# The warp's offsets stored as one-byte integers

## The chip, the cores and the metric

One core of a Trainium2 chip. The metric is the device time of one execution, in microseconds.

## What is computed

The input is x, 128 images of 64 x 256. Four layers follow one another, each x + ffn(cond(x)):

```python
x = x + _L0_ffn_ref(_L0_cond_ref(x, dx, angle), ...)      # rigid transform of each image, ternary-weight FFN
x = x + _L1_ffn_ref(_L1_cond_ref(x, ..., ids), ...)       # masked attention, mixture of 4 experts, 2 per row
x = x + _L2_ffn_ref(_L2_cond_ref(x, ids, ...), ...)       # language adapter and layer norm, frequency-domain product
x = x + _L3_ffn_ref(_L3_cond_ref(x, ids, W, b), ...)      # per-category product, gated ternary-weight FFN
```

The change concerns the rigid transform alone. Each output pixel is read at a rotated and shifted place with bilinear weights:

```python
ix = (yp / h * 2.0 + 1.0) * 0.5 * (w - 1);  iy = (xp / w * 2.0 + 1.0) * 0.5 * (h - 1)
out = gather(iy0, ix0) * (wy0 * wx0) + gather(iy0, ix1) * (wy0 * wx1)
    + gather(iy1, ix0) * (wy1 * wx0) + gather(iy1, ix1) * (wy1 * wx1)
```

## The kernel before

The 128 images are worked in 32 quarters of 4 (QI = 4, NQ = 32). A quarter goes through four parts on the same engines: the front (warp, FFN of layer 0, attention and router of layer 1), the experts (rows sorted by expert, in ten blocks of quarters), the back (adapter, layer norm, frequency product) and the last part (category product, gated FFN). On each engine these parts are threads of instructions; `weave` merges them in an order that is written out by hand as a string per engine (`ORDER`). An engine works its string strictly in that order, and engines wait for one another by semaphores.

The warp of one image runs like this. An image is cut into groups of GJ x GI = 4 x 8 = 32 output pixels, so that a pixel of a group is one of 32 places k. For each group a window of the padded input is gathered by GpSimd into SBUF (`w_win`, line 1158, four indirect DMAs an image). Inside a window, place k of every group of an image reads a 3 x 3 patch at one offset, the same for all groups. The 32 offsets of an image are the array `w_offsets`: `shift[k]` is row shift times WY plus column shift, with WY = 4, computed once for all images.

In `prepare`, VectorE computes the offsets of all images with the image index on the partition (line 424) as an array of PX = 32 integers; SyncE stores it to DRAM (`offD`, line 334). In `network`, SyncE reloads the 128 offsets of a quarter into partition 0 of `woff[par]` (`load_offsets`, line 586), in two buffers by turns, with semaphore `s_off`. In thread `warp(q)` (lines 762 to 795) VectorE's sequencer loads the 32 offsets of one image into 32 of its registers with one TENSOR_LOAD (lines 770 to 773), and then issues 32 multiplications (line 780), one for each place k, whose input address is `shift[k] + a * IWIN` from the register; a short register operation (FUSED_REGOPS) goes ahead of each. After that come the sums over the patch (lines 784, 785, 789, 790, 795). Between groups of 8 multiplications, and between the sums, the written order takes VectorE to instructions of the other threads. The registers are rewritten for the next image.

Two more loads of VectorE and the others into registers are of single integers: the expert's column (line 983 on VectorE, 1327 on ScalarE, 630 on SyncE), all of four bytes.

Of the kernel before, what the change touches and what calls it, by code (L numbers as in the profile page):

```python
# [12 lines left out]
FP8 = mybir.dt.float8e4  # L13
U32 = mybir.dt.uint32
I32 = mybir.dt.int32
ALU = mybir.AluOpType
ACT = mybir.ActivationFunctionType
AX = mybir.AxisListType

B, S, D, F = 128, 64, 256, 1024  # L20
# [13 lines left out]
PX = GJ * GI  # L34
# [4 lines left out]
QI = 4  # L39
# [200 lines left out]
def build(nc, t, out):  # L240

    with ExitStack() as ctx:
        def sb(name, cols, dt=F32, c=ctx):
            return c.enter_context(nc.sbuf_tensor(name, [P, cols], dt))

        def sem(name):
            return ctx.enter_context(nc.semaphore(name))


        cst = sb("const", CCONST)  # L250
        idb = sb("ident_f16", P, F16)
        wq = {n: sb(n + "_ternary", 2 * F, FP8) for n in BITW}
        wmean = sb("weight_means", len(BITW))
        moe2 = sb("moe_w2", EXP * NFB * D)
        moeb1 = sb("moe_b1", EXP * NFB)
        router = sb("router", NDB * EXP)
        brB = sb("router_bias", EXP)
        b1B = sb("L0_b1_rows", F)
        b2B = sb("L0_b2_rows", D)
        fbB = sb("freq_bias_rows", D)  # L260
        attW = sb("att_W1", NDB * ADIM)
        attb = sb("att_b1", 1)
        attv = sb("att_v", P)
        freqM = sb("freq_matrix", NDB * D)
        KB = sb("moe_offset_rows", EXP * D)
        ones = sb("ones", P)
        ids = sb("image_ids", 3 * B, I32)
        nhalf = sb("minus_half", TT)
        hmag = sb("half_magic", 1)
        frD = nc.dram_tensor("w_frac_all", (P, 2 * B * NG), F32, kind="Internal").ap()  # L270
        fdD = nc.dram_tensor("w_shift_frac_all", (2 * B * PX,), F32, kind="Internal").ap()
        idxD = nc.dram_tensor("w_idx_all", (P, B * NG), U32, kind="Internal").ap()
        offD = nc.dram_tensor("w_offsets_all", (1, B * PX), I32, kind="Internal").ap()
        XS = nc.dram_tensor("moe_in_sorted", (2 * ARENA, D), F32, kind="Internal").ap()
        YS = nc.dram_tensor("moe_out_sorted", (2 * ARENA, D), F32, kind="Internal").ap()
        XMD = nc.dram_tensor("x_middle", (TOK, D), F32, kind="Internal").ap()

        psum = [ctx.enter_context(nc.psum_tensor(f"bank{i}", [P, 512], F32)) for i in range(8)]
        PA, PB, PT, PM, H0, H1, Y0, Y1 = psum

        s_raw = [sem(f"p_raw{i}") for i in range(len(BITW))]
        s_ld = sem("p_ld")
        network(nc, t, out, locals())


def prepare(nc, t, g):

    cst, moe2, moeb1, router, brB, b1B, b2B, fbB, attW, attb, attv, ones, ids, nhalf, hmag, frD, fdD, idxD, offD = (g[k] for k in
        ("cst", "moe2", "moeb1", "router", "brB", "b1B", "b2B", "fbB", "attW", "attb", "attv", "ones", "ids", "nhalf", "hmag",
         "frD", "fdD", "idxD", "offD"))  # L290
# [3 lines left out]
    with ExitStack() as ctx:  # L294
        def sb(name, cols, dt=F32):
            return ctx.enter_context(nc.sbuf_tensor(name, [P, cols], dt))
# [13 lines left out]
        fd = sb("w_shift_frac", 2 * PX)  # L310
        low = sb("w_shift_floor", 2 * PX)
        idx = sb("w_idx", B * NG, U32)
        woff = sb("w_offsets", PX, I32)
        dI, dJ = sb("w_shift_i", 2 * GI), sb("w_shift_j", 2 * GJ)
        s_v, s_trig, s_sin, s_set, s_w, s_geo, s_out = [
            sem("p_" + n) for n in ("dve_steps", "trig", "sin", "ones", "warp_ld", "geometry", "geometry_out")]
# [39 lines left out]
        def _(dve):  # L356
# [9 lines left out]
            v.tensor_copy(trig[:, 2 * B:2 * B + 1], pcol[:, :])  # L366
            v.tensor_scalar(trig[:, 2 * B + 1:TR], pcol[:, :], 1.5707963267948966, None, ALU.add)
            ch.link(v.tensor_scalar(trig[:, B:2 * B], ang, 1.5707963267948966, None, ALU.add))
            t01, t23 = trig[:, 0:TR], trig[:, TR:2 * TR]
            ch.link(v.tensor_scalar(t23, t01, 0.15915494309189535, MAGIC, ALU.mult, ALU.add))  # L370
            ch.link(v.tensor_scalar(t23, t23, MAGIC, None, ALU.subtract))
            ch.link(v.scalar_tensor_tensor(t01, t23, -6.28125, t01, ALU.mult, ALU.add))
            ch.link(v.scalar_tensor_tensor(t01, t23, -0.0019353071795864769, t01, ALU.mult, ALU.add))
            v.tensor_scalar(t01, t01, -3.1415925, 3.1415925, ALU.max, ALU.min).then_inc(s_trig, 1)
# [53 lines left out]
def network(nc, t, out, g):  # L428
    cst, idb, wq, wmean, moe2, moeb1, router, brB = (g[k] for k in
        ("cst", "idb", "wq", "wmean", "moe2", "moeb1", "router", "brB"))  # L430
    b1B, b2B, fbB, attW, attb, attv, freqM, KB, ones, ids, nhalf, hmag, frD, fdD, idxD, offD, XS, YS, XMD = (g[k] for k in
        ("b1B", "b2B", "fbB", "attW", "attb", "attv", "freqM", "KB", "ones", "ids", "nhalf", "hmag", "frD", "fdD", "idxD",
         "offD", "XS", "YS", "XMD"))
# [7 lines left out]
    with ExitStack() as ctx:  # L441
        def sb(name, cols, dt=F32):
            return ctx.enter_context(nc.sbuf_tensor(name, [P, cols], dt))
# [7 lines left out]
        fr = [sb(f"w_frac{i}", 2 * QI * NG) for i in range(2)]  # L451
        fd = [sb(f"w_shift_frac{i}", 2 * QI * PX) for i in range(2)]
        idx = [sb(f"w_idx{i}", QI * NG, U32) for i in range(2)]
        woff = [sb(f"w_offsets{i}", QI * PX, I32) for i in range(2)]
        H = sb("w_hat", 2 * QPX * TAP)
        HY = QPX * TAP
        M = sb("w_prod", IPX * TAP * TAP)
# [24 lines left out]
        pl = sb("plan_work", 5 * VIRT + EXP + 1 + 2 * TILES + 2 * VIRT * TILES + TILES + 1)  # L482
        plan = sb("plan", 4 * GT, I32)
        A2h = sb("adapter_hidden_T", QT)
# [20 lines left out]
        wsum = sb1("weight_sums", len(BITW))  # L505
        wscale = sb1("weight_scales", len(BITW))
        prepare(nc, t, {**g, **locals()})
        first.close()

# [1277 lines left out]
```

## Time and profile before

| | |
|---|---|
| median of 3 runs | 2598.43 us (2594.84 to 2608.49) |
| span of the profiled execution | 2589.5 us |
| PE, DVE, ACT, POOL busy in it | 2086.4, 1789.4, 1646.5, 989.8 us |

The span is the profiled execution's own time from the first to the last instruction; the median of the runs is 8.9 us above it. PE is the matrix engine, DVE VectorE, ACT ScalarE, POOL GpSimd. "DVEq", "ACTq" and "SPq" rows are work of an engine's sequencer, which isn't counted as busy. "Issue" as the releaser of a wait means that the engine waited for nothing that the profile shows as an engine's or a DMA's work.

### The profile page before, as it was taken

How to read it: one execution, taken by the hardware profiler on the slowest of the kernel's cores; microseconds unless marked ns; L12 is line 12 of the kernel's file. 1: busy time of each engine (PE TensorE's matmuls, PEld its weight loads, DVE VectorE, ACT ScalarE, POOL GpSimd, SP SyncE). 2: the span in 40 equal slices, each digit the busy share in tenths (PEclk: the TensorE clock that was granted, in tenths of full speed). 3: DMA queues.
4: the chain of work that ended last, by engine and by line, in shares of the span. 5: the costliest groups of instructions: out<-in, count | busy, mean ns of one | idle time of the engine just before them, and what ended most of it. 6: DMA issues, size and time to landing. Idle time of an engine off the chain costs nothing. (4 is left out here: it accounts for less than half of the span.)

```text
span 2589.5 us, 50733 instructions
## 1 busy us (share of the span) xinstructions
PE 2086.4 (81%) x12000; PEld 1611.2 (62%) x12000; DVE 1789.4 (69%) x7954; ACT 1646.5 (64%) x2802; POOL 989.8 (38%) x1092
## 2 busy tenths in 40 slices
PE   1054698788888888888898889989888899999975
PEld 1022476566766666666676667767666777777842
DVE  3677876677777777777787778787878564544344
ACT  1025555566777777777677677778676587767552
POOL 0345444644354444444444444454444221221010
PEclk8565698998999999998999999999999999999977
DMA  7623344434445545535455454655564445355531
GB/s 291 232 54 82 112 123 130 136 118 137 125 145 173 151 145 154 161 112 156 130 184 156 141 146 147 183 151 144 164 175 137 131 143 164 120 170 176 157 96 53
DMA packets 291315, 375.94 MB, mean 145 GB/s; under 512 B 127138, under 2 KB 234055, under 8 KB 276044
## 3 DMA queue, kind: packets, MB, share of 16 engines
q1 hardware_dynamic: 260016, 297.02, 37.5%
q0 software_dynamic: 28672, 68.21, 9.3%
q10 hardware_dynamic: 2332, 7.47, 0.7%
q8 instruction: 100, 1.64, 0.3%
q14 instruction: 195, 1.60, 0.2%
HBM read 291.23 MB, written 72.93 MB: 141 GB/s over the span
## 5 line engine op out<-in xcount | busy, mean ns | idle before, releaser
L1158 POOL DMA_INDIRECT w_win<-in_windows,w_idx x512 | 527.6, 1030 | 839.6 <-DMA w_win<-in_windows,w_idx 653.1
L780 DVE TENSOR_TENSOR w_prod<-w_win,w_hat 128x36 f32<-128x36 f32 x4096 | 529.5, 219 | 285.8 <-issue 282.9
L1549 PE MATMUL bank<-moe_w,moe_hidden_T 128*128 x2528 | 642.3, 395 | 23.8 <-DVE moe_y L991 14.0
L1533 PE MATMUL bank<-moe_xT,moe_w_tile 128*128 128x256 f32 (+1 forms) x3008 | 635.2, 355 | 6.4 <-ACT moe_xT L1318 4.9
L1533 PEld LDWEIGHTS bank<-moe_xT,moe_w_tile 128*128 128x128 f32 x3008 | 513.1, 195 | 82.1 <-issue 12.3
L1549 PEld LDWEIGHTS bank<-moe_w,moe_hidden_T 128*128 128x128 f32 x2528 | 473.4, 196 | 102.6 <-issue 40.5
L1335 ACT ACTIVATE moe_hidden_T<-bank,moe_b 128x256 f32<-128x256 f32 (+1 forms) x752 | 288.0, 436 | 176.5 <-PE bank L1533 129.2
L1335 ACT ACT_TABLE_LOAD x151 | 193.7, 1283 | 74.9 <-PE bank L1533 57.7
L1178 POOL DMA_INDIRECT moe_in_sorted<-c,rows x128 | 136.4, 1066 | 252.0 <-DVE rows L921 102.0
L1192 POOL DMA_INDIRECT moe_y_back<-moe_out_sorted,rows_back x128 | 125.3, 979 | 271.9 <-DMA moe_y_back<-moe_out_sorted,rows_back 149.2
L1077 DVE SCALAR_TENSOR_TENSOR hidden_back<-bank,back_stats,hidden_back 128x512 f32<-128x512 f32 x128 | 95.2, 744 | 103.7 <-ACT hidden_back L1375 103.4
L1375 ACT ACT_TABLE_LOAD x117 | 150.1, 1283 | 2.3
L1425 PE MATMUL bank<-L_w_ternary,q1T_front 128*128 128x512 fp8e4 x256 | 84.3, 414 | 63.7 <-DVE hidden_front L830 58.9
L1243 ACT ACTIVATE w_hat<-w_t 128x512 f32<-128x512 f32 x64 | 40.2, 628 | 121.8 <-DVE w_out L795 113.1
L1425 PE MATMUL bank<-L_gate_ternary,q1T_back 128*128 128x512 fp8e4 x256 | 82.7, 407 | 30.5 <-DVE hidden_back L1077 22.4
L1261 ACT ACTIVATE hidden_front<-hidden_front 128x1024 f32<-128x1024 f32 x64 | 67.9, 1060 | 61.9 <-DVE hidden_front L830 56.1
L830 DVE SCALAR_TENSOR_TENSOR hidden_front<-bank,front_stats,L_b_rows 128x512 f32<-128x512 f32 x128 | 95.1, 743 | 14.3 <-PE bank L1425 8.7
L1305 ACT ACTIVATE q_back<-hidden_back,half_magic,back_tile_stats 128x1024 f16<-128x1024 f32 x64 | 79.5, 1242 | 37.8 <-DVE back_tile_stats L1084 36.1
L1305 ACT ACTIVATE q_front<-hidden_front,half_magic,front_tile_stats 128x1024 f16<-128x1024 f32 x64 | 79.3, 1240 | 37.9 <-DVE front_tile_stats L836 28.4
L1375 ACT ACTIVATE hidden_back<-bank,back_stats 128x512 f32<-128x512 f32 x128 | 88.0, 687 | 20.4 <-PE bank L1425 18.5
L1011 DVE SCALAR_TENSOR_TENSOR x_back<-moe_y_back,gates_back,x_back 128x256 f32<-128x256 f32 x128 | 55.9, 478 | 52.1 <-issue 20.2
L991 DVE TENSOR_TENSOR moe_y<-bank,moe_offset_rows 128x512 f32<-128x512 f32 (+1 forms) x94 | 56.5, 601 | 47.1 <-PE bank L1549 30.7
(260 smaller groups left out, 3748.2 us busy)
## 6 DMA issues: line engine op xcount, KB each, us to landing
moe_w_tile<-in_moe_w SPq DMA_DIRECT2D x94, 1024.0 KB
L_cond_W<-in_L_cond_W SPq DMA_DIRECT2D x128, 256.0 KB
adapters<-in_adapter SPq DMA_DIRECT2D x128, 192.5 KB
gamma_beta<-in_gamma_beta SPq DMA_DIRECT2D x128, 128.0 KB
moe_x<-moe_in_sorted SPq DMA_DIRECT2D x64, 256.0 KB
moe_out_sorted<-moe_y SPq DMA_DIRECT2D x64, 256.0 KB
x_front<-in_x SPq DMA_DIRECT2D x32, 256.0 KB
w_win<-in_windows,w_idx POOLq DMA_INDIRECT x512
```

The costliest lines, as they stand in the source:

```text
L780: ins = v.tensor_tensor(out3, win, hy, ALU.mult)
L830: v.scalar_tensor_tensor(HBA[:, n * 512:(n + 1) * 512], A0[:, :], sa[:, DQ][:, one(u)], b1B[:, n * 512:(n + 1) * 512], ALU.mult, ALU.add). ...
L1077: v.scalar_tensor_tensor(hb, B1[:, :], sbk[:, DQ][:, one(u)], hb, ALU.mult, ALU.mult).then_inc(E["b_hb"], 1)
L1158: gp.indirect_dma_start(out=V[:, g_ * WLEN:(g_ + 1) * WLEN], out_offset=None, in_=t["windows"], in_offset=bass.IndirectOffsetOnAxis(ap=idx ...
L1178: gp.indirect_dma_start(out=XS, out_offset=bass.IndirectOffsetOnAxis(ap=pos[par][:, c:c + 1], axis=0), in_=C1[:, u * D:(u + 1) * D], in_of ...
L1192: gp.indirect_dma_start(out=YG[:, c * D:(c + 1) * D], out_offset=None, in_=YS, in_offset=bass.IndirectOffsetOnAxis(ap=posb[:, c:c + 1], ax ...
L1305: return s.activation(to[:, :], hidden[:, :], ACT.Identity, bias=hmag[:, :], scale=scale)
L1335: ins = s.activation(hT[:, (f % (2 * FPU)) * TILE:(f % (2 * FPU)) * TILE + width(n)], (H0, H1)[r % 2][:, (f % FPU) * TILE:(f % FPU) * TILE ...
L1375: s.activation(HBB[:, n * 512:(n + 1) * 512], B0[:, :], ACT.Silu, scale=sbk[:, 6 * TT + u:6 * TT + u + 1]).then_inc(E["b_silu"], 1)
L1425: last = te.matmul(bank[:, :], q1t[:, d * QT + u * P:d * QT + (u + 1) * P], w[:, d * F + n * 512:d * F + (n + 1) * 512], start=(d == 0), s ...
L1533: last = te.matmul((H0, H1)[r % 2][:, (f % FPU) * TILE:(f % FPU) * TILE + width(n)], W1[n % 3][:, d * F + f * P:d * F + (f + 1) * P], XT[: ...
L1549: last = te.matmul(Y[:, u * D:(u + 1) * D], hT[:, (f % (2 * FPU)) * TILE + u * P:(f % (2 * FPU)) * TILE + (u + 1) * P], ap(moe2, weight + ...
```

## The change

The element type of the offsets becomes an unsigned one-byte integer in all three places: the array in `prepare`, the DRAM tensor and the two buffers in `network`. The instructions, their order and their semaphores stay.

```diff
@@ -13,6 +13,7 @@
 U32 = mybir.dt.uint32
 I32 = mybir.dt.int32
+U8 = mybir.dt.uint8
@@ -270,7 +271,7 @@
-        offD = nc.dram_tensor("w_offsets_all", (1, B * PX), I32, kind="Internal").ap()
+        offD = nc.dram_tensor("w_offsets_all", (1, B * PX), U8, kind="Internal").ap()
@@ -310,7 +311,7 @@
-        woff = sb("w_offsets", PX, I32)
+        woff = sb("w_offsets", PX, U8)
@@ -451,7 +452,7 @@
-        woff = [sb(f"w_offsets{i}", QI * PX, I32) for i in range(2)]
+        woff = [sb(f"w_offsets{i}", QI * PX, U8) for i in range(2)]
```

## Rows read from the trace of the kernel before

**Rows 1.** The page: span, busy time, and the span in 40 equal slices.

```profile
span 2589.5 us, 50733 instructions
PE 2086.4 (81%) x12000; PEld 1611.2 (62%) x12000; DVE 1789.4 (69%) x7954; ACT 1646.5 (64%) x2802; POOL 989.8 (38%) x1092
...
PE   1054698788888888888898889989888899999975
...
DVE  3677876677777777777787778787878564544344
```

**Rows 2.** Busy time of each engine by stretch (times in us, count of instructions).

```profile
core 0: us, PE busy (x) PEld busy (x) DVE busy (x) ACT busy (x) POOL busy (x), PEclk, DMA share, GB/s
60.00:400.00 340.00, 172.30 (x747) 113.65 (x748) 245.12 (x1221) 128.76 (x229) 146.98 (x154) 0.65 0.40 125
400.00:2000.00 1600.00, 1385.55 (x8131) 1090.24 (x8130) 1237.84 (x5830) 1140.04 (x1965) 733.11 (x808) 0.96 0.50 148
2000.00:2500.00 500.00, 468.61 (x2830) 370.59 (x2828) 244.42 (x753) 342.25 (x556) 94.77 (x112) 0.98 0.48 149
```

**Rows 3.** DVE's longest waits, 400 to 2000 us: total us, times, longest.

```profile
DVE w_prod L780 <- issue: 194.4, 123, 3.1
DVE front_tile_stats L839 <- POOL front_tile_stats L1199: 34.5, 18, 6.7
DVE c_adapter L1043 <- POOL mean_var L1199: 31.0, 11, 7.6
DVE front_stats L822 <- POOL front_stats L1199: 13.1, 6, 4.8
```

**Rows 4.** Tile w_offsets, 400 to 2000 us: the register load; duration ns min/median/max.

```profile
L771 DVEq TENSOR_LOAD <-w_offsets x100: 2096/2104/3009, 409.9 to 1993.7; - x100
```

**Rows 5.** PE's longest waits for DVE, 400 to 2000 us.

```profile
PE bank L1413 <- DVE c_adapter L1043: 45.6, 13, 7.2
PE bank L1425 <- DVE hidden_front L830: 27.6, 20, 3.6
...
PE bank L1425 <- DVE hidden_back L1077: 12.6, 7, 5.8
PE bank L1413 <- DVE x_back L1011: 12.4, 4, 8.0
```

**Rows 6.** Tile w_offsets, whole span: making and storing the offsets.

```profile
L424 DVE SCALAR_TENSOR_TENSOR w_offsets<-w_shift_floor x1: 184/184/184, 25.7 to 25.7; 128x32 int32<-128x32 f32 x1
...
DMA to landing us min/median/max: 1.9/1.9/1.9
```

**Rows 7.** DMA issues: the reload of a quarter's offsets.

```profile
w_offsets<-w_offsets_all SPq DMA_DIRECT2D x32, 0.5 KB
```

**Rows 8.** Line 780, 400 to 2000 us: register operation and multiplication.

```profile
L780 DVEq FUSED_REGOPS  x3200: 3/57/731, 400.9 to 1999.2; - x189
L780 DVE TENSOR_TENSOR w_prod<-w_win,w_hat x3200: 182/217/1370, 401.8 to 1999.4; 128x36 f32<-128x36 f32 x189
```

**Rows 9.** Tile plan, whole span: loads of a single register on three sequencers.

```profile
L1327 ACTq TENSOR_LOAD <-plan x376: 272/278/749, 305.3 to 2478.6; - x188
...
L630 SPq TENSOR_LOAD <-plan x94: 177/268/1208, 297.5 to 2457.4; - x94
L983 DVEq TENSOR_LOAD <-plan x94: 289/309/889, 329.4 to 2481.3; - x94
```

**Rows 10.** Timeline of DVE, 1000 to 1060 us: start, us, instruction, [idle before].

```profile
1008.67 1.00 DVE L780 TENSOR_TENSOR w_prod<-w_win,w_hat 128x36 f32<-128x36 f32 x7 [2.48 <-issue]
1009.93 0.22 DVE L780 TENSOR_TENSOR w_prod<-w_win,w_hat 128x36 f32<-128x36 f32 x1 [0.26 <-issue]
...
1030.15 1.13 DVE L780 TENSOR_TENSOR w_prod<-w_win,w_hat 128x36 f32<-128x36 f32 x8 [1.19 <-issue]
...
1050.77 1.12 DVE L780 TENSOR_TENSOR w_prod<-w_win,w_hat 128x36 f32<-128x36 f32 x8 [2.36 <-issue]
```

**Rows 11.** Tile w_offsets: the register loads of 60 to 400 us and from 2000 us on.

```profile
L771 DVEq TENSOR_LOAD <-w_offsets x26: 2098/2103/7698, 63.1 to 391.5; - x26
...
L771 DVEq TENSOR_LOAD <-w_offsets x2: 2101/2102/2103, 2014.7 to 2028.2; - x2
```

**Rows 12.** DVE's waits before line 780, 60 to 400 us, then whole span.

```profile
DVE w_prod L780 <- issue: 84.3, 31, 20.8
...
DVE w_prod L780 <- issue: 282.9, 157, 20.8
```

**Rows 13.** PE's longest waits, 60 to 400 us.

```profile
PE bank L1667 <- DVE weight_sums L1110: 85.0, 4, 30.5
PE bank L1425 <- DVE hidden_front L830: 31.3, 10, 9.2
```

## The prediction

> **What bounds the kernel now.** I read the page's first two parts, then busy time by stretch, then what DVE and PE wait for in each stretch. The rows are of one profiled execution of 2589.5 us [rows 1]. The 40-slice rows show three stages [rows 1]: a start in which PE is little used, a long middle with PE at 8 to 9 tenths and DVE at 7 to 8, and an end in which PE stays at 9 and DVE falls to 4 or 5. Busy time by stretch puts numbers on them [rows 2]. From 60 to 400 us DVE is busy 245.12 of 340 us, PE 172.30. From 400 to 2000 us PE is busy 1385.55 of 1600 us (86.6%) and DVE 1237.84 (77%). From 2000 to 2500 us PE is busy 468.61 of 500 us (93.7%), DVE 244.42: the warp is over there and PE is the bound.
>
> PE looks like the bound of the middle too, but the waits say otherwise. DVE's longest wait there is not for an engine: 194.4 us before w_prod (line 780), put down to "issue" [rows 3]. What DVE's sequencer does in those places is the register load of line 771: 100 TENSOR_LOADs in this stretch, of 2104 ns in the median and 2096 at the least [rows 4]. The next 32 multiplications take their window addresses from these registers, so nothing behind the load can be issued until it ends, though the engine itself is idle. Busy time plus this wait is 1237.84 + 194.4 = 1432 us, 90% of the stretch; the next largest waits are the round trips to POOL, 34.5, 31.0 and 13.1 us, and PE appears in the first rows not at all [rows 3]. PE on the other hand waits mostly for DVE: 45.6 us for c_adapter, 27.6 for hidden_front, 12.6 and 12.4 for hidden_back and x_back [rows 5]. So DVE with its loads sets the pace from 60 to 2000 us, with PE 8 or 9% behind it, and PE alone sets it after that.
>
> **The change part by part.**
>
> *Stores and DMAs of offsets.* The DVE instruction that makes the offsets (line 424) writes 32 bytes a partition in place of 128; it runs once, 184 ns, and the store (line 334) is one DMA that lands in 1.9 us [rows 6]. The 32 reloads (line 586) carry 0.5 KB each [rows 7], now 0.125 KB; they are issued a quarter ahead, and no wait for them is among DVE's waits [rows 3]. Nothing: at most a few tenths of a microsecond either way, once. The quarters' cover, should it go, costs one landing of about 1.9 us per quarter. Largest offset: (33-3)*4+4-3 = 121, so one byte holds it, and the registers hold the same numbers; the 57 ns of register arithmetic per multiplication [rows 8] stay.
>
> *The load itself.* 128 loads of 32 registers become 128 loads of 32 registers from a quarter of the bytes. Their new price is the one thing that the trace doesn't show, so I bound it. DVE's own load of a single register (line 983) takes 309 ns; SP's takes 268 and ACT's 278 [rows 9]. A load of 32 takes 2104. If each register were fetched by itself at nearly the single price, 32 would take 8 us or more; so either several registers come with one fetch, or the fetches overlap and each further register costs (2104 - 309)/31 = 58 ns. In the first form 128 bytes come in n equal pieces of (2104 - 309)/(n - 1) each. A piece can't cost more than the whole single load of 309, so n is 7 or more: with 8 pieces (16 bytes each) 256 ns a piece, with 16 pieces 120 ns, with 32 pieces 58 ns. 32 one-byte offsets are then 2, 4 or 8 pieces: 309 + 256 = 565, 309 + 3 x 120 = 669, or 309 + 7 x 58 = 715 ns. In the second form the price goes by registers and stays 2104. At the far end, one-byte elements aren't grouped at all: 309 + 31 x 256 = 8245 ns. [...] The gain is 2104 - 565 = 1539 ns a load.
>
> [...]
>
> *How much of it DVE feels.* A part of a load is hidden behind work already queued. In the timeline the idle before the first w_prod of an image is 2.48, 1.19 and 2.36 us in three neighbours, and 0.26 us before a w_prod that follows no load [rows 10]. On the average of the middle: 123 waits hold 194.4 us; 23 of them are such short ones, 23 x 0.26 = 6, which leaves 188 us for 100 loads, 1.88 us each. A load with nothing to hide it leaves about 2.4 [rows 10]; so some 0.5 us are hidden on the average, and with 565 ns, 2.4 - 1.54 - 0.5 or about 0.4 us would still show. DVE gains 1.5 us a load: 150 us in the middle. From 60 to 400 us 26 loads [rows 11] gain 1.5 each, 39 us; the wait before L780 is 84.3 us there, of which 20.8 is one wait at the start of the network that has another cause [rows 12].
>
> *How much reaches the end.* What is late next is PE. In the middle it has 1385.55 us of work; at the 93.7% it holds once DVE is out of the way, that is 1385.55/0.937 = 1479 us, so no more than 121 of the 150 us can be had. DVE would stand at about 1450 of that by its own sum, so the two are within 2% of each other, and engines in a written order lose time to each other then. I take three quarters of 121: 90 us (PE at 91.8% of 1510 us, a little under the later stage). Bounds: half of the 121, 60 us, and the whole of DVE's 150. From 60 to 400 us PE isn't near its limit, DVE is the bound, and PE waits for DVE there in its longest rows [rows 13]; of 39 us I take 30, bounds 15 and 39. After 2028 us there is no load [rows 11]: nothing.
>
> Sum: 90 + 30 = 120 us off 2589.5, which is 2469.5 for the profiled span. The median of the runs (2598.43) is 8.9 us above the span, so **2478 us**. The bounds give 2598.4 - 75 = 2523 and 2598.4 - 189 = 2409; with 669 or 715 ns for the load the gain is a tenth smaller, inside them. This case's own range is 2405 to 2530.
>
> **The rivals.**
>
> *One-byte elements are fetched one by one (slower).* The grouping of registers that makes 32 of them cost 2104 ns may hold for four-byte elements alone. Then a load is 8245 ns, 6.1 us more; 128 x 6.14 = 786 us more on DVE's sequencer, which is the bound already. DVE's other waits in the middle (34.5 + 31.0 + 13.1 for POOL and smaller ones) would take up some 100 of it: about 2598 + 690 = 3290 us. It turns slower, by over 0.5%, where a load takes 2.2 us or more: 13 us in all are 0.1 us a load. For it: all loads of this trace are of four bytes, so nothing shows that the grouping goes by bytes. [...]
>
> *The price goes by registers (no change).* 58 ns for each register, as the handling of one register by a sequencer could well take: the register arithmetic of line 780 has just this median, 57 ns [rows 8]. Then the load stays at 2104 ns, the change does not do what it is for, and the time is 2598 +- 7. Against it: 309 ns for one register would then be mostly a fixed part of 250.
>
> *The load is short, but the gain stays on DVE.* If PE's order keeps it waiting in the same places, only the start (15 to 30 us) and a third of the middle (40) come through: 2530 to 2545. PE's waits for DVE in the middle, 45.6 + 27.6 + 12.6 + 12.4 and more, speak against it.
>
> **How the numbers follow.** The load is shortened and the gain comes through: 0.63, 2478 us. Shortened, with little of it at the end: 0.06, 2535 us. Unchanged load: 0.14, 2598 us. One by one: 0.17, 3290 us. Faster by over 0.5% (13 us; about what a measurement of this kernel can tell from no change) is the first two, 0.69; within it 0.14; slower 0.17. The first three hold 0.83 together, so the range reaches from 2405 to 2606 and leaves out the fourth.
>
> **What would show it.** The TENSOR_LOAD of line 771 in the profile after: 565 ns by my reading (669 or 715 for smaller pieces), 2104 for the second rival, 8.2 us for the first. The wait of DVE before line 780: from 282.9 us to about 90. From 400 us to the end of the warp PE's share rises from 86.6% to 91 or 92%; its waits for DVE fall by half. After the warp nothing changes but the start time. The prediction is wrong in its size if the wait before line 780 falls as told and waits of DVE for PE or POOL grow by as much, and wrong altogether if the load isn't shorter.

## The result and the profile after

The changed kernel takes 3125.02 us (median, 3115.53 to 3130.34) against 2603.46 us for the kernel before, measured beside it: ratio 1.198, 95% interval 1.194 to 1.202. It is 20% slower. That is outside the range and in the direction of the first rival, the one by one.

The page of the changed kernel, span, busy time and 40 slices (what rows 1 show of before):

```profile
span 3123.6 us, 50733 instructions
PE 2243.7 (72%) x12000; PEld 1717.4 (55%) x12000; DVE 1778.0 (57%) x7954; ACT 1649.9 (53%) x2802; POOL 978.9 (31%) x1092
...
PE   1143377677777787778777777787877879899975
...
DVE  3555555555656666656565656665656654454344
```

The instructions are as many as before and DVE is busy as long (1778.0 against 1789.4 us); only the time between them has grown. The next rows are those of the tile w_offsets in the same kernel: its register load, the reload and the making of the offsets (duration ns min/median/max). They answer [rows 4, 6]:

```profile
L772 DVEq TENSOR_LOAD <-w_offsets x128: 7103/7160/18090, 64.5 to 2552.2; - x128
L587 SPq DMA_DIRECT2D w_offsets<-w_offsets_all x32: 277/366/690, 36.6 to 2451.8; - x32
L425 DVE SCALAR_TENSOR_TENSOR w_offsets<-w_shift_floor x1: 185/185/185, 25.5 to 25.5; 128x32 uint8<-128x32 f32 x1
...
DMA to landing us min/median/max: 1.9/1.9/1.9
```

The load takes 7160 ns in place of 2104. The making of the offsets takes 185 ns against 184 and the store still lands in 1.9 us. The single four-byte load of line 984 takes 311 ns (309 before). Next come DVE's waits of the changed kernel, 400 to 2000 us (total us, times, longest), to be read against [rows 3], and PE's longest ones there, against [rows 5]; "PE bank" is a PE instruction that writes one of its output buffers:

```profile
DVE w_prod L781 <- issue: 576.3, 98, 7.9
DVE hidden_front L831 <- PE bank L1426: 10.1, 8, 2.6
```

```profile
PE bank L1550 <- DVE moe_y L992: 72.5, 15, 7.3
PE bank L1426 <- DVE hidden_front L831: 59.4, 16, 7.3
PE bank L1426 <- DVE hidden_back L1078: 30.9, 10, 5.7
```

Two things are to be seen. The wait before w_prod is 576 us of 1600, at 7.9 us at most, and DVE's waits for POOL, 34.5 and 31.0 us before, are gone from the first rows. Busy time and this wait are 966.18 + 576.3 = 1542 us, 96% of the stretch: DVE with its loads is the bound. And PE, which waits for it, waits up to 7.3 us at a time in these rows, as long as a load. Busy time by stretch (columns as in [rows 2]):

```profile
60.00:400.00 340.00, 103.43 (x368) 56.73 (x369) 182.09 (x883) 80.68 (x137) 105.15 (x112) 0.54 0.30 96
400.00:2000.00 1600.00, 1196.72 (x6305) 934.48 (x6304) 966.18 (x4659) 885.33 (x1543) 581.72 (x647) 0.87 0.39 114
```

PE falls from 1385.55 to 1196.72 us of 1600, and its granted clock, a mean over the stretch, from 0.96 to 0.87 of full speed. Over the whole span PE's 12000 matmuls take 2243.7 us in place of 2086.4. In that stretch this isn't on the bound, which is DVE.

Sum: 128 x (7.16 - 2.10) = 647 us more on DVE's sequencer, 522 us at the end. Why 125 us of it don't reach the end is the subject of the second half of the experiments.

### The profile page after: what moved, and what is told of

It is laid out like the page before. It is cut to its first block and busy times, and to the rows that moved or that the text cites. A ratio compares the mean times of both kernels' runs of the same rounds, so it can differ in the third digit from the quotient of the medians.

```text
span 3123.6 us, 50733 instructions
## 1 busy us (share of the span) xinstructions
PE 2243.7 (72%) x12000; PEld 1717.4 (55%) x12000; DVE 1778.0 (57%) x7954; ACT 1649.9 (53%) x2802; POOL 978.9 (31%) x1092
## 5 line engine op out<-in xcount | busy, mean ns | idle before, releaser
L1159 POOL DMA_INDIRECT w_win<-in_windows,w_idx x512 | 512.3, 1001 | 926.9 <-DMA w_win<-in_windows,w_idx 571.9
L1550 PE MATMUL bank<-moe_w,moe_hidden_T 128*128 x2528 | 692.7, 418 | 86.2 <-DVE moe_y L992 79.1
L1534 PE MATMUL bank<-moe_xT,moe_w_tile 128*128 128x256 f32 (+1 forms) x3008 | 677.3, 372 | 12.4 <-ACT moe_xT L1319 11.6
L1550 PEld LDWEIGHTS bank<-moe_w,moe_hidden_T 128*128 128x128 f32 x2528 | 510.5, 212 | 177.5 <-issue 104.1
L1534 PEld LDWEIGHTS bank<-moe_xT,moe_w_tile 128*128 128x128 f32 x3008 | 545.4, 207 | 99.1 <-ACT moe_xT L1319 17.6
L1179 POOL DMA_INDIRECT moe_in_sorted<-c,rows x128 | 134.1, 1048 | 370.8 <-issue 161.3
L1426 PE MATMUL bank<-L_w_ternary,q1T_front 128*128 128x512 fp8e4 x256 | 93.6, 454 | 137.6 <-DVE hidden_front L831 129.6
L1426 PE MATMUL bank<-L_gate_ternary,q1T_back 128*128 128x512 fp8e4 x256 | 89.4, 436 | 81.1 <-DVE hidden_back L1078 70.4
L1262 ACT ACTIVATE hidden_front<-hidden_front 128x1024 f32<-128x1024 f32 x64 | 67.8, 1059 | 125.9 <-DVE hidden_front L831 103.8
L1426 PEld LDWEIGHTS bank<-L_w_ternary,q1T_front 128*128 128x128 bf16 x256 | 22.4, 105 | 170.8 <-DVE hidden_front L831 149.1
L1420 PE MATMUL bank<-ident_f,q_front 128*128 128x128 f16 x512 | 47.5, 247 | 92.7 <-DVE x_front L929 45.1
L831 DVE SCALAR_TENSOR_TENSOR hidden_front<-bank,front_stats,L_b_rows 128x512 f32<-128x512 f32 x128 | 95.3, 744 | 16.9 <-PE bank L1426 15.8
```

What stands on the lines that cost most here:

```text
L831: v.scalar_tensor_tensor(HBA[:, n * 512:(n + 1) * 512], A0[:, :], sa[:, DQ][:, one(u)], b1B[:, n * 512:(n + 1) * 512], ALU.mult, ALU.add). ...
L1159: gp.indirect_dma_start(out=V[:, g_ * WLEN:(g_ + 1) * WLEN], out_offset=None, in_=t["windows"], in_offset=bass.IndirectOffsetOnAxis(ap=idx ...
L1179: gp.indirect_dma_start(out=XS, out_offset=bass.IndirectOffsetOnAxis(ap=pos[par][:, c:c + 1], axis=0), in_=C1[:, u * D:(u + 1) * D], in_of ...
L1426: last = te.matmul(bank[:, :], q1t[:, d * QT + u * P:d * QT + (u + 1) * P], w[:, d * F + n * 512:d * F + (n + 1) * 512], start=(d == 0), s ...
L1534: last = te.matmul((H0, H1)[r % 2][:, (f % FPU) * TILE:(f % FPU) * TILE + width(n)], W1[n % 3][:, d * F + f * P:d * F + (f + 1) * P], XT[: ...
L1550: last = te.matmul(Y[:, u * D:(u + 1) * D], hT[:, (f % (2 * FPU)) * TILE + u * P:(f % (2 * FPU)) * TILE + (u + 1) * P], ap(moe2, weight + ...
```

## The experiments

**Where the price of the load comes from.** The first run leaves everything at four bytes but the load itself:

```diff
-                    first = woff[par][0:1, a * PX:(a + 1) * PX]
+                    first = woff[par][0:1, a * PX:(a + 1) * PX].bitcast(U8)[:, 0:4 * PX:4]
```

> The kernel before with everything left at four bytes (arithmetic, DRAM tensor, DMAs, tile); only the register load reads the low byte of each word, 32 one-byte elements 4 bytes apart. Theory (one-byte elements are fetched one by one, 221 ns each, wherever they lie): the TENSOR_LOAD takes 7.16 us as in the changed kernel and the run about 3125 us. Rival (the narrow stores, the DMAs or the packed bytes of the changed kernel cost the time): the load is back at 2.1 us and the run at 2600 us.

Measured: 3117.28 us (one execution), and the load

```profile
L772 DVEq TENSOR_LOAD <-w_offsets x128: 7107/7158/19371, 62.7 to 2548.6; - x128
```

The loss is in the load's element type: with the stores, the DRAM tensor and the DMAs at four bytes it is all there.

The second takes two-byte elements in the changed kernel:

```diff
-U8 = mybir.dt.uint8
+U8 = mybir.dt.uint16
```

> The changed kernel with two-byte elements in place of one-byte ones, in all three places. Theory (fetches are shared by four-byte elements alone): the load takes 7.16 us again and the run 3125 us. Rival A (only single bytes are fetched alone; two-byte ones are shared in pieces of 16 bytes): 4 pieces, about 311 + 3 x 221 + some 0.2 = 1.2 us, and the run at 2500 us. Rival B (the price goes by some width-dependent step, half the elements sharing): 3.7 us.

Measured: 3117.54 us (one execution), load 7153 ns. Both rivals of that text fall.

The third keeps four bytes and moves each row one word on:

```diff
-        woff = [sb(f"w_offsets{i}", QI * PX, I32) for i in range(2)]
+        woff = [sb(f"w_offsets{i}", QI * PX + 4, I32) for i in range(2)]
 ...
-                sp.dma_start(woff[par][0:1, :], offD...
+                sp.dma_start(woff[par][0:1, 1:1 + QI * PX], offD...
 ...
-                    first = woff[par][0:1, a * PX:(a + 1) * PX]
+                    first = woff[par][0:1, 1 + a * PX:1 + (a + 1) * PX]
```

> The kernel before, its four-byte offsets stored one word further on in the tile, so that each row of 32 begins 4 bytes past a multiple of 16 bytes. Theory (sharing needs four-byte elements and nothing else): 9 pieces in place of 8, 2.3 us a load, the run at 2600 to 2620 us. Rival (a fetch is shared only in a row that begins at a multiple of 16 bytes; otherwise each element comes by itself): 7.16 us a load and 3125 us.

Measured: 3131.78 us (one execution), and

```profile
L771 DVEq TENSOR_LOAD <-w_offsets x128: 7123/7196/18384, 65.1 to 2555.5; - x128
```

My theory fell here: four bytes are not enough. In these runs the cheap price (2104 ns for 32) came only with words in a row that begins at the right place; one word off costs as much as one byte wide (7196 and 7160 ns). Which multiple is the right one this run doesn't tell, as the rows of before begin at multiples of 128 bytes from the tile's start. A later run bounds it: the second load of `bytes_8_of_32` begins 32 bytes past such a multiple and has the cheap price (24 words, 1597 ns at the least, 1601 in the median). So 32 bytes are enough; whether 16 or 8 are, no run shows.

**What the load's time is worth at the end.** The fourth run puts the load at the price that I had forecast:

```diff
-                    first = woff[par][0:1, a * PX:(a + 1) * PX]
+                    first = woff[par][0:1, a * PX:a * PX + GI]
 ...
-                        win = ap(V, shift[k] + a * IWIN, ...
+                        win = ap(V, shift[k % GI] + a * IWIN, ...
```

> The kernel before, but each image loads only its first 8 offsets and every row of 8 multiplications uses these, so 24 of the 32 places are read at a wrong offset; the multiplications are as many and as large as before. It puts the load at about the price that the forecast gave the one-byte load. Pieces of 16 bytes at 221 ns and some 8 ns for each register: 311 + 221 + 8 x 8, about 590 ns. Forecast's step (DVE sets the pace until 2000 us, 121 us at most before PE binds, three quarters of it had): about 120 us faster, ratio 0.954, wait before line 780 from 283 to about 90 us. Rival (PE takes the bound over at once, or its order keeps it waiting): 15 to 60 us faster, ratio 0.98 to 0.995.

Measured: 2573.0 us against 2593.07, ratio 0.991 (0.988 to 0.994): 20 us, where my step gave 120. The load is 597 ns. Tile w_offsets, then DVE's longest waits of this kernel, 400 to 2000 us:

```profile
L771 DVEq TENSOR_LOAD <-w_offsets x128: 591/597/2133, 63.0 to 2011.2; - x128
```

```profile
DVE front_tile_stats L839 <- POOL front_tile_stats L1199: 91.3, 31, 10.0
DVE c_adapter L1043 <- POOL mean_var L1199: 72.8, 15, 10.7
DVE front_stats L822 <- POOL front_stats L1199: 25.1, 6, 12.5
...
DVE w_prod L780 <- issue: 16.9, 46, 0.8
```

Against [rows 3] the wait before w_prod fell by 177.5 us (194.4 to 16.9), and the three waits for POOL rose by 110.6 (78.6 to 189.2). Most of the idle time that DVE lost before w_prod came back as waits for POOL. What POOL did meanwhile, its longest wait of the same kernel and stretch:

```profile
POOL w_win L1158 <- DMA w_win<-in_windows,w_idx: 514.1, 228, 5.8
```

In thread `gather`, GpSimd waits for the landing of one of an image's four gathers before it issues the next. The square roots that DVE wants stand behind these waits in GpSimd's written order. The waits can be left out without a race, since VectorE waits for all four before it reads the windows (line 765), and SyncE before it overwrites the indices (line 575):

```diff
                         if g_ == a * NG:
                             after(pool, E["part"], QI * (q - 1) + a + 1)
-                        else:
-                            pool.wait_ge(s_win[a], 16 * (NG * q + g_ - a * NG))
```

> The kernel before without GpSimd's wait, inside an image, for the landing of the gather before the next of its four gathers. With 8 registers DVE's waits for POOL's square roots grew from 79 to 189 us in the stretch from 400 to 2000 us, while POOL stood in line behind waits for w_win's DMA (482 and 514 us there). Theory (POOL's queue with these waits is as late as DVE is, so that taking them away alone leaves DVE with its loads as the bound): DVE's waits for POOL fall to under 30 us in that stretch and the time by 10 to 60 us. Rival (the gathers' DMAs overlap and slow each other or the other transfers, or the waits were idle time that cost nothing): within 10 us of before.

Measured: 2472.62 us against 2596.58, ratio 0.949 (0.945 to 0.953): 124 us, twice the upper end of what I expected and more than the load's cut gave. The register loads of this kernel over the whole span, then DVE's waits, 400 to 2000 us:

```profile
L771 DVEq TENSOR_LOAD <-w_offsets x128: 2096/2106/7891, 48.5 to 1913.9; - x128
```

```profile
DVE w_prod L780 <- issue: 192.3, 118, 2.8
DVE c_adapter L1043 <- POOL mean_var L1197: 27.8, 13, 4.8
...
DVE front_tile_stats L839 <- POOL front_tile_stats L1197: 11.1, 10, 2.5
```

In this stretch the loads are as exposed as before (192.3 against 194.4), and the waits for POOL fell by four tenths (the two largest 38.9 against 65.5, not under 30 as I had said). These waits are not the whole gain. DVE's busy time in the stretch rose from 1237.84 to 1274.20 us, so the same work takes an estimated 47 us less there. Some of the rest stands at the start: the first load begins at 48.5 us in place of 63.1 [rows 11], and the wait before w_prod from 60 to 400 us is 55.6 us in place of 84.3 [rows 12].

Was the load's cut worth 20 us because POOL stood in the way, or is the load's idle time worth no more in any case? Both cuts together decide:

> Both cuts together: 8 registers loaded in place of 32 (so 24 of 32 places are read at a wrong offset, with as many multiplications as before), and no wait of GpSimd for the landing of one gather before the next of an image. Alone they gave 20 us and 124 us. Theory (DVE with its loads and POOL with its gather waits were both about as late, so the load's cut was stopped by POOL; with the gathers free the load's cut now reaches the end until PE binds): DVE's 192 us before line 780 in 400 to 2000 us fall to under 30, and the time from 2473 to 2400 to 2440 us, ratio to the kernel before 0.925 to 0.94. Rival (the load's idle time is worth nothing beyond 20 us, whatever POOL does): 2453 us or more, ratio 0.945 or more.

Measured: 2401.94 us, ratio 0.927 (0.923 to 0.931), 71 us below free gathers alone. The same cut of the load was worth 20 us with POOL's waits in place. Busy time by stretch of this kernel:

```profile
400.00:2000.00 1600.00, 1481.56 (x8883) 1182.05 (x8884) 1290.74 (x5955) 1240.14 (x2112) 753.76 (x823) 0.98 0.54 161
```

PE is at 1481.56 of 1600, 92.6% (with free gathers alone it had been 1454.16, 90.9%): here it comes near the 93.7% that I had taken for the limit.

**A dearer load.** Two loads in place of one, as an intermediate price:

```diff
+                    _, shift = nc.values_load_multi_w_load_instructions(woff[par][0:1, a * PX:(a + 1) * PX], ...)
                     for k in range(PX):
```

> The kernel before with each image's register load issued twice in a row: 2 x 2104 = 4.2 us in place of 2.1. With load prices of 0.6, 2.1 and 7.2 us the time was 2573, 2593 and 3117 to 3125 us, so a microsecond of load cost 10 us below and 104 us above, where all of it would be 128. Theory (below some price the other engines hide the load, above it DVE's sequencer is the bound and every microsecond costs nearly 128): the bend lies at about 3.0 us a load, 4.2 us give 2593 + 1.2 x 128 = 2740 to 2750 us. Rival (no bend, a constant share of about 0.8 of each microsecond reaches the end from 2.1 us on): 2593 + 2.1 x 104 = 2810 us.

Measured: ratio 1.0005 (0.9972 to 1.0039), and the trace has 128 loads of 2104 ns, not 256:

```profile
L774 DVEq TENSOR_LOAD <-w_offsets x128: 2097/2104/7629, 64.5 to 2034.4; - x128
```

Line 774 is the second of the two; the first, whose registers nobody reads, isn't in the program that ran. The run says nothing on the bend; it is a second measurement of the kernel before. The bend was then sought with loads whose values are all used, nb = 8 and 16:

```diff
-                    first = woff[par][0:1, a * PX:(a + 1) * PX]
-                    _, shift = nc.values_load_multi_w_load_instructions(first, ...)
+                    _, few = nc.values_load_multi_w_load_instructions(
+                        woff[par][0:1, a * PX:a * PX + nb].bitcast(U8)[:, 0:4 * nb:4], ...)
+                    _, rest = nc.values_load_multi_w_load_instructions(
+                        woff[par][0:1, a * PX + nb:(a + 1) * PX], ...)
+                    shift = tuple(few) + tuple(rest)
```

> The kernel before, but the first 8 offsets of an image are loaded as single bytes of their words, the other 24 as words: two loads. By the prices found so far (95 ns fixed, 211 a fetch, 10 a register) 1.86 + 1.60 = 3.5 us in place of 2.1. Theory with a bend (idle engines hide a part, then every microsecond of load costs 128 us; bend near 3.1 us): 2593 + 50 = 2640 us, ratio 1.02. Rival (104 us for every microsecond from 2.1 us on): 2593 + 142 = 2735 us, ratio 1.055.

> The same with 16 offsets as bytes and 16 as words: 3.63 + 1.10 = 4.7 us a load. Theory with a bend near 3.1 us: 2593 + 210 = 2803 us, ratio 1.08. Rival without a bend: 2593 + 273 = 2866 us, ratio 1.105.

Measured: 2655.99 us, ratio 1.023 (1.019 to 1.028), and 2788.34 us, ratio 1.075 (1.070 to 1.079). Their loads, tile w_offsets of the one and then of the other:

```profile
L771 DVEq TENSOR_LOAD <-w_offsets x128: 1831/1841/7253, 64.5 to 2094.3; - x128
L775 DVEq TENSOR_LOAD <-w_offsets x128: 1597/1601/5511, 71.8 to 2096.2; - x128
```

```profile
L771 DVEq TENSOR_LOAD <-w_offsets x128: 3593/3611/14201, 64.5 to 2225.2; - x128
L775 DVEq TENSOR_LOAD <-w_offsets x128: 1094/1098/1511, 78.8 to 2228.8; - x128
```

The five prices give a curve. The time is 2597 us times the ratio; the slope is between a row and the one above it:

| load of an image, us | ratio | slope, us of time for each us of load (128 if all of it counts) |
|---|---|---|
| 0.60 | 0.991 | |
| 2.10 | 1 | 16 |
| 3.44 | 1.023 | 45 |
| 4.71 | 1.075 | 105 |
| 7.16 | 1.198 | 131 |

By the intervals of the ratios each slope is uncertain by 5 to 12. There is a bend, as the theory had it, and it is a round one: from 4.7 us on every microsecond counts in full, below 2.1 us an eighth of it does. The rival of a constant share is out at both points.

**Two ways to a cheaper load with right offsets.** Four loads of 8 words, one ahead of each row of multiplications:

```diff
                     for k in range(PX):
                         if k and k % GI == 0:
                             yield
+                        if k % GI == 0:
+                            _, shift = nc.values_load_multi_w_load_instructions(
+                                woff[par][0:1, a * PX + k:a * PX + k + GI], ...)
-                        win = ap(V, shift[k] + a * IWIN, ...
+                        win = ap(V, shift[k % GI] + a * IWIN, ...
```

> The kernel before, correct offsets, four loads of 8 registers in place of one of 32, each just ahead of the row of 8 multiplications that uses it. A load of 8 was 0.597 us, so 4 x 0.6 = 2.4 us of sequencer time an image against 2.1, but each piece can hide behind the instructions of other threads that are queued before its row. Theory (DVE's idle time before line 780 shrinks from 283 to 100 to 180 us, and POOL or PE take over at once, as they did with 8 registers): 0 to 20 us faster, ratio 0.992 to 1.0. Rival (the longer total of 2.4 us is what counts): 0 to 30 us slower.

> Free gathers with correct offsets and four loads of 8 registers, each just ahead of its row of multiplications. Split alone halved DVE's wait before the multiplications (283 to about 140 us) and gave 12 us. Theory: with POOL out of the way it gives about half of what the cut to 8 registers gives, 15 to 40 us below free gathers alone: 2430 to 2457 us, ratio 0.935 to 0.947. Rival: the same as free gathers alone, 2473 us, ratio 0.95.

Measured: alone 2584.64 us, ratio 0.995 (0.992 to 0.997); with free gathers 2473.62 us, ratio 0.955 (0.951 to 0.959), no better than free gathers alone (0.949). The rival of the second text holds. (The wait for issue with split loads alone was 154.3 us, not the 140 of that text.) DVE's time by line in the kernel with both: busy us, mean ns, idle us before it and what ended it:

```profile
L781 DVE TENSOR_TENSOR w_prod<-w_win,w_hat 128x36 f32<-128x36 f32 x4096 | 568.2, 224 | 170.8 <-issue 134.1 <-DVE w_cols L786 13.2 <-DVE router_logits L890 5.4
```

The wait for issue went from 254.8 us (free gathers) to 134.1, but w_prod itself is busy 568.2 us where it was 527.1, and other short waits before it add 37 us where they were 3. Of 121 us some 46 are left. Why these don't reach the end stays open.

The other way keeps the one-byte offsets, loads them as 8 words, and takes each out by shift and mask:

```diff
-                    first = woff[par][0:1, a * PX:(a + 1) * PX]
+                    first = woff[par][0:1, a * PX:(a + 1) * PX].bitcast(I32)
-                    _, shift = nc.values_load_multi_w_load_instructions(first, ...)
+                    _, four = nc.values_load_multi_w_load_instructions(first, ...)
 ...
+                        shift_k = (four[k // 4] >> (8 * (k % 4))) & 255
```

> The changed kernel (one-byte offsets in all three places), but the 32 bytes of an image are loaded as 8 four-byte words, and each multiplication's offset is taken out of its word by a shift and a mask in the register arithmetic ahead of it. The load falls to 0.6 us. The register arithmetic ahead of each multiplication was 57 ns, with a multiplication every 120 ns. Theory (it grows to 100 to 170 ns and spaces the 4096 multiplications out by 0 to 80 ns): DVE loses 0 to 330 us there, gains 190 us at the load; 2570 to 2720 us. Rival (the arithmetic is hidden whole behind the multiplications): as with 8 registers, 2573 us.

Measured: 2706.79 us, ratio 1.040 (1.037 to 1.044). Line 782 of this kernel, its register instructions and then its multiplications by line as above, followed by the multiplications of the kernel before (line 780):

```profile
L782 DVEq ALU_OP  x7168: 40/45/57, 66.6 to 2157.8; - x200
L782 DVEq FUSED_REGOPS  x4096: 46/57/71, 66.7 to 2157.9; - x196
L782 DVE TENSOR_TENSOR w_prod<-w_win,w_hat 128x36 f32<-128x36 f32 x4096 | 818.9, 225 | 239.8 <-issue 89.5
```

```profile
L780 DVE TENSOR_TENSOR w_prod<-w_win,w_hat 128x36 f32<-128x36 f32 x4096 | 529.5, 219 | 285.8 <-issue 282.9
```

The load is 597 ns, 193 us less over the 128 images, but 7168 more register instructions of 45 ns, 323 us, come on the same sequencer: 130 us more by this count. On DVE itself it is more. The multiplications and the idle time before them take 818.9 + 239.8 = 1059 us where they took 529.5 + 285.8 = 815, which is 243 us more or 1.9 us an image. Of these 110 reach the end. That agrees with the table: a load of 2.1 + 1.9 = 4.0 us lies between its rows of 3.44 and 4.71 us, and so does the ratio of 1.040. Why the register instructions cost DVE more than their own durations no run shows.

## Why the prediction was wrong

*The load's price* is the step that failed first. I had derived from [rows 4, 9] that a load of 32 words comes in pieces, and went on from 8 pieces of 16 bytes each to 32 bytes in two pieces. The traced loads held only words, in rows that begin at round addresses. The 565 ns in the sum were my choice among estimates, and no run shows them for 32 one-byte elements: the change's load measured 7160 ns. What comes near them is a load of the same 32 bytes as 8 words, 597 ns. Six loads now fit one line, 95 ns + 211 ns a fetch + 10 ns a register, where a fetch is a term of the fit that no row shows: 1 word 1 fetch (316, measured 309 to 311), 8 words 2 fetches (597, 597), 16 words 4 (1099, 1098), 24 words 6 (1601, 1601), 32 words 8 (2103, 2104), 32 bytes 32 (7167, 7160). The three constants were fitted to the loads of 8, 32 words and 32 bytes; the others test them, as do 8 bytes (1863, 1841) and 16 bytes (3631, 3611). That four words share a fetch went into the fit and doesn't come out of it. Every row of words that was loaded has one or a multiple of 8 of them, and 95 ns + 181 ns for every 8 words + 40 ns a register gives the same numbers within 5 ns. So pieces of 16 bytes are neither shown nor ruled out against pieces of 32; a load of 4 words, 436 ns by the second line and 346 by the first, would decide. What is shown is that the cheap price was a matter of words, and of their place, and not of bytes. No row of before held a narrow element, so none spoke against the one-by-one rival, and its 0.17 was an estimate without a row behind it. For each register a load of 32 took 7160/32 = 224 ns with one-byte elements, 7196/32 = 225 ns with words out of place and 2104/32 = 66 ns with aligned words.

*The first rival's size.* It had 8245 ns for a load, since I took the whole difference between one and 32 words as fetches of 256 ns; between 16 and 32 one-byte elements each costs (7160 - 3611)/16 = 222 ns (211 + 10 by the fit). With 7160 ns its own sum is 128 x 5.06 = 647 us, less the 100 it let other waits take up, about 3145 us: the measured 3125 is that. Its direction and its place were right, and that the price goes by elements (1841, 3611 and 7160 ns for 8, 16 and 32 of one byte); its price for a load was 15% too high.

*The offsets' store and reload at nothing* held: they took 185 ns and 1.9 us after, and the run with byte loads of words alone lost as much.

*How much reaches the end* failed as well, and the right price would have hidden it. With the load that I forecast, the time is 20 us less, not 120. The step that broke is the reading of [rows 3]: I called the 34.5, 31.0 and 13.1 us for POOL round trips and named PE as next late. POOL was. (PE wasn't "8 or 9% behind" by the sum used for DVE either: 1385.55 beside 1432 us is 3%; the 8% are 1479 beside the stretch's 1600.) POOL's busy time, 733.11 us of 1600 [rows 2], looks harmless, and I hadn't added its own waits. The same stretch of the kernel before, POOL's waits for its own DMAs and for issue:

```profile
POOL w_win L1158 <- DMA w_win<-in_windows,w_idx: 481.9, 219, 6.7
...
POOL moe_y_back L1192 <- DMA moe_y_back<-moe_out_sorted,rows_back: 66.9, 34, 5.6
POOL w_win L1158 <- issue: 56.0, 162, 4.4
POOL moe_in_sorted L1178 <- DMA moe_in_sorted<-c,rows: 47.9, 29, 5.0
...
POOL moe_in_sorted L1178 <- issue: 35.1, 65, 6.1
POOL moe_y_back L1192 <- issue: 18.6, 45, 2.1
```

Busy 733, the DMAs 482 + 67 + 48 and issue 56 + 35 + 19 are 1440 us, 90% of the stretch, as much as DVE's 90% with its loads. Taking away most of DVE's part (20 us), POOL's (124 us) and both (195 us, more than their sum of 144) shows that each held the other's gain back, and that POOL's part alone was worth more. The steps that worked were DVE's idle time saved by a short load (177.5 us in the middle; I had 150) and the 93.7% that I took as PE's limit, to which it came within 1.1 points, at 92.6%, once POOL had been freed.

*The third rival*, a short load whose gain stays on DVE, was the right case for the second half: I had it at 2530 to 2545 us and 0.06, for the wrong reason (PE's order), and the run with the short load took 2573 us.

## What to carry to other kernels

A price derived from rows of one element type and one alignment holds for these; before a layout is narrowed to save bytes, find a row with the narrow element. And when an engine's busy time plus its own stalls makes it the bound, add up the same sum, busy and waits for transfers, for every other engine: an engine with 46% busy time held the kernel back at least as much as the one that I had named. What a cut is worth can be measured before a way to make it is found, by a run that loads 8 offsets and leaves the other 24 out.

## What the runs showed of the hardware

A load of 32 registers from SBUF by VectorE's sequencer takes 2.1 us for aligned four-byte elements, 7.15 to 7.16 us for one-byte or two-byte ones and 7.20 us for words 4 bytes out of place. That is some 222 ns for each further one-byte element ((7160 - 3611)/16), and 63 ns for each further aligned word ((2104 - 597)/24); whether words share a fetch, and how many, four or eight, isn't shown. A shift or a mask in a register on that sequencer takes 45 ns (median of 7168). Unpacking four values from each word made the kernel 110 us slower than loading 32 words, yet with 2706.79 us it is well below the 3125.02 of one-byte loads. And of the changes that compute the same result, one outside the question was the best: without the waits between an image's gathers the kernel takes 2472.62 us, 5% less than before.
